# First layer of an audio tower: the attention's out-projection computed from high and low parts, with new steps on ScalarE, VectorE and TensorE

## The reference

```
h = tok(x)                                     # pairs of tokens -> 188 tokens, conv as a product, layer norm
h = h + attn0(layernorm(h))                    # 16 heads of 16; the softmax runs over the batch axis (64)
h = h + ffn0(layernorm(h))                     # 256 -> 704 -> 256, inputs, weights and hidden rounded to FP4 by blocks of 16
h = h + attn1(layernorm(h))                    # linear attention, 16 heads of 64
h = h + ffn1(h)                                # 256 -> 1024 -> 256, integer weights
# end of attn0:
out = out.transpose(1, 0, 2).reshape(L, N, inner)
out = einsum('lni,ei->lne', out, out_proj) + out_bias
```

## Time and profile before

| what | value |
|---|---|
| median of 3 runs | 4551.7 us (4547.76 to 4551.86) |
| the profiled execution's own time | 4539.33 us |
| its span in the profile | 4536.7 us |
| TensorE matmuls busy over the span | 4354.9 us, 96% |
| TensorE weight loads | 3972.3 us, 88% |
| DVE | 3317.8 us, 73% |
| ACT | 2712.1 us, 60% |
| POOL | 2100.0 us, 46% |

### The profile page before, as it was taken

One profiled execution on the slowest core, in us unless ns is written; L12 is line 12 of the kernel. 1 busy time (PEld: TensorE's weight loads), 2 busy tenths in 40 slices (PEclk: granted clock), 3 DMA queues, 4 the chain that ended last, 5 costly groups with the idle time before them and its releaser, 6 DMA issues.

```text
span 4536.7 us, 121660 instructions
## 1 busy us (share of the span) xinstructions
PE 4354.9 (96%) x43948; PEld 3972.3 (88%) x43948; DVE 3317.8 (73%) x7106; ACT 2712.1 (60%) x5662; POOL 2100.0 (46%) x2682
## 2 busy tenths in 40 slices
PE   5999999999999958999999999999999999999997
PEld 4889999999899848899999999999999999989996
DVE  6999999999999845666666666666666666666665
ACT  4777777777777734555555555555555555545553
POOL 4566666666666522433433443343343344334333
PEclk8999999999999979999999999999999999999998
DMA  2100000000000010000000000000000000000000
GB/s 71 43 24 24 24 24 24 23 22 24 24 24 24 21 45 5 5 15 8 9 15 9 9 12 12 9 11 13 9 9 15 9 9 14 10 9 8 15 5 11
DMA packets 64982, 79.21 MB, mean 17 GB/s; under 512 B 8800, under 2 KB 51168, under 8 KB 64480
## 3 DMA queue, kind: packets, MB, share of 16 engines
q1 hardware_dynamic: 64608, 74.07, 5.6%
HBM read 49.40 MB, written 24.64 MB: 16 GB/s over the span
## 4 chain that ended last, share of the span: by engine, by line
PE 56%; DVE 3%; issue 2%; ACT 1%; POOL 1%; ACTq 0%; DVEq 0%; POOLq 0%
PE bA L1093 11%; PE bA L1095 9%; PE bA L1094 9%; PE bS L1398 4%; PE bO L1420 3%; PE bA L1484 3%; PE bB L1093 2%; PE bB L1094 2%; PE bB L1384 2%; PE bB L1095 2%; PE bB L1383 2%; PE bA L1485 2%; PE bT L1436 2%; PE bO L1424 1%; PE bO L1429 1%
## 5 line engine op out<-in xcount | busy, mean ns | idle before, releaser
L1820 POOL TENSOR_TENSOR sqs_lo<-sq,sqs_hi 128x768 fp32r<-128x768 f32 x256 | 480.6, 1878 | 673.9 <-ACT sqs_hi L1535 670.1
L1634 DVE TENSOR_TENSOR qk_lo<-bA,qk_hi 128x384 fp32r<-128x384 f32 x512 | 284.3, 556 | 517.1 <-ACT qk_hi L1535 516.8
L1554 ACT ACTIVATE phi<-bB 128x768 f32<-128x768 f32 x256 | 207.4, 810 | 662.5 <-PE bB L1384 662.5
L1778 POOL TENSOR_TENSOR yT_lo<-tanh_y,yT_hi 128x384 fp32r<-128x384 f32 x256 | 259.3, 1013 | 545.0 <-ACT yT_hi L1535 545.0
L1535 ACT ACTIVATE qk_hi<-bA 128x384 fp32r<-128x384 f32 x512 | 251.9, 492 | 195.2 <-PE bA L1095 188.0
L1644 DVE TENSOR_TENSOR aT<-bS,mask 128x1024 f32<-128x1024 f32 x256 | 311.0, 1215 | 1.3 <-PE bS L1403 1.3
L1544 ACT ACTIVATE sq<-bA 128x384 f32<-128x384 f32 x512 | 250.2, 489 | 62.1 <-DVE qk_lo L1634 61.3
L571 ACT ACTIVATE kblk<-gu,kb_masked,rowmask 128x128 f32<-128x128 f32 x752 | 271.7, 465 | 5.1 <-PE gu L452 5.0
L1093 PE MATMUL bA<-fc_lo,yT_hi 128*128 128x256 f32 x768 | 230.7, 300 | 13.1 <-POOL yT_lo L1778 6.4
L1093 PE MATMUL bA<-wv_lo,xT_hi 128*128 128x256 f32 x768 | 230.0, 300 | 5.9 <-ACT sq L1544 1.3
L1093 PE MATMUL bA<-wo_lo,attT_hi 128*128 128x256 f32 x768 | 226.3, 295 | 9.8 <-ACT sq L1544 2.1
(11 more groups left out here) (269 smaller groups left out, 16222.6 us busy)
## 6 DMA issues: line engine op xcount, KB each, us to landing
xT<-in_x SPq DMA_DIRECT2D x94, 256.0 KB, 2.6
h_scratch<-h SPq DMA_DIRECT2D x188, 64.0 KB, 1.9
hx<-h_scratch SPq DMA_DIRECT2D x32, 256.0 KB, 2.7
out<-res SPq DMA_DIRECT2D x32, 256.0 KB, 2.2
hx<-h_scratch SPq DMA_DIRECT2D x64, 64.0 KB, 2.4
out<-res SPq DMA_DIRECT2D x64, 60.0 KB, 1.8
q<-in_fc_q SPq DMA_DIRECT2D x2, 1024.0 KB, 7.7
wq_sb<-in_wq SPq DMA_DIRECT2D x1, 1024.0 KB, 5.0
```

The source lines that it names most:

```text
L1634: dve.tensor_tensor(dst, src, hi.bitcast(fp32), ALU.subtract).then_inc(S[done], 1)
L1778: pool.tensor_tensor(yT[1][:, f % RING, :], tanh_y[f % 2][:], yT[0][:, f % RING, :].bitcast(fp32), ALU.subtract).then_inc(S["y_lo"], 1)
L1820: pool.tensor_tensor(sqs[1][:], sq[:], sqs[0][:].bitcast(fp32), ALU.subtract).then_inc(S["sq_lo"], 1)
```

## The change

`attT` becomes a pair, `attT_hi` and `attT_lo`, in fp32r, and so does the out-projection's weight, `outw_hi` and `outw_lo`, made once from `outw_sb`: the high part by ACT at the end of slot 0, the low part by DVE in slot 1. In every slot ACT's `att_copy` writes `attT_hi` and stands ahead of the tanh of half 0 in place of behind it. A new DVE step, `att_low`, subtracts it from the transposes in PSUM into `attT_lo`; it stands behind `score_shift` and ahead of `glu_gate` of half 0, and raises `attT_split`. The out-projection waits for `attT_split` and calls `product3` twice. All who waited for `attT_copied` to reuse the PSUM bank now wait for `attT_split`.

```
-        attT = sb("attT", [128, KC, 128])
+        attT = sb("attT_hi", [128, KC, 128], fp32r), sb("attT_lo", [128, KC, 128], fp32r)
+        outw = sb("outw_hi", [128, KC, DM], fp32r), sb("outw_lo", [128, KC, DM], fp32r)
...
 def xq_transpose(t):
-                              [("attT_copied", t - 3, 1, 1), ("xqT_split", t - 4, 1, 1)])
+                              [("attT_split", t - 3, 1, 1), ("xqT_split", t - 4, 1, 1)])
 def att_transpose(t):
-                              [("ln1T_copied", t - 1, 1, 1), ("attT_copied", t - 3, 1, 1)])
+                              [("ln1T_copied", t - 1, 1, 1), ("attT_split", t - 3, 1, 1)])
 def outproj(t):
-                    wait(pe, "attT_copied", t - 1)
+                    if isinstance(t, int) and t == 2:
+                        pe.wait_ge(wout_lo, 1)
+                    wait(pe, "attT_split", t - 1)
                     for c in range(KC):
-                        last = pe.matmul(cv[:, 0:DM], attT[:, c, :], outw_sb[:, c, :], start=c == 0, stop=c == KC - 1)
+                        last = product3(pe, cv[:, 0:DM], [x[:, c, :] for x in attT], [x[:, c, :] for x in outw],
+                                        c == 0, c == KC - 1)
 def ln1_transpose(t):
-                    bank_free(pe, t, [("attT_copied", t - 2, 1, 1)],
+                    bank_free(pe, t, [("attT_split", t - 2, 1, 1)],
...
 ACT, att_copy:
-                    copy(attT[:], tp[:, 0:256], "attT_copied")
+                    copy(attT[0][:], tp[:, 0:256].rearrange("p (c t) -> p c t", c=KC), "attT_copied")
 ACT, slot:
+                    if exists(t, 2):
+                        att_copy(t)
                     if exists(t, 3):
                         tanh(t - 3, 0)
-                    if exists(t, 2):
-                        att_copy(t)
                     if exists(t, 0):
                         ln0_normalize(t)
...
                     if isinstance(t, int) and t == 0:
+                        act.wait_ge(wout, 32)
+                        act.activation(outw[0][:], outw_sb[:], ACT.Copy).then_inc(wout_hi, 1)
                         weight_magnitude("up")
...
 DVE:
+                def att_low(t):
+                    wait(dve, "attT_copied", t - 1)
+                    dve.tensor_tensor(attT[1][:], tp[:, 0:256].rearrange("p (c t) -> p c t", c=KC), attT[0][:].bitcast(fp32),
+                                      ALU.subtract).then_inc(S["attT_split"], 1)
 DVE, slot:
                         score_shift(t - 1, s_st)
+                    if exists(t, 2):
+                        att_low(t)
                     if exists(t, 3):
                         glu_gate(t - 3, 0)
                         glu_up(t - 3, 0)
...
                     if isinstance(t, int) and t == 1:
+                        dve.wait_ge(wout_hi, 1)
+                        dve.tensor_tensor(outw[1][:], outw_sb[:], outw[0][:].bitcast(fp32), ALU.subtract).then_inc(wout_lo, 1)
                         dve.wait_ge(S["rs1"], 4 * 2)
                         weight_round("up")
```

## The result

The change made the kernel slower, by 0.6%. Its median is 4578.59 us (4577.03 to 4582.4, 4 runs) beside 4550.93 us for the kernel before (4547.76 to 4551.86, 4 runs): ratio 1.0063, interval 1.0046 to 1.0081, that is 27.7 us. The prediction had 22.7 us more and 4574.

A forecast was written before the change was run, and what follows sets the result against it. A tie between DVE's ring and TensorE's was taken to bound the kernel; 91 slots x 0.24 = 21.9, with slot 2 22.7 us more: 4562.0 from the profiled execution, 4574.4 from the median; 8 in 10 range 4558 to 4592.

The forecast's parts named there:

- DVE's ring: Loop slot: closed chain from `rowmax` through DVE, POOL, ACT and the scores back to `rowmax`; `att_low` adds net 0.24 us.
- The pitch and its cover: `att_low` on DVE: 0.34 us start to start, less 0.10 us covered by the wait for the up products.
- TensorE's saving: Out-projection: six fp32r products for four fp32 pieces save 0.16 us per tile, if TensorE waited for nothing.
- its new wait: TensorE waits for `att_low` before the out-projection, starting near 913.95 in place of 913.70; costs nothing beyond the ring.
- the other kind of slot: Slots where DVE waits for the up products; out-projection slips about 0.1 us, more than made good.
- ACT's order: `attT`'s copy ahead of tanh(0) delays `ln0_normalize` and what follows on ACT by 0.10 us, hidden: nothing.
- slot 2: Before the loop: TensorE waits for `att_low` behind `P`, so `up_hi` moves 0.8 us later; other end nothing.
- the weights: Splitting the out-projection weight on ACT in slot 0 and DVE in slot 1 fits in idle time: nothing.
- TensorE's busy share: Sign in the profile between 300 and 1500 us: down by about 2 points, with a new idle before `q_sb`.
- TensorE as the bound: Rival: DVE has room, so every tile saves 0.16 us, 15 us in all, 4537 us; chance 0.10.
- The tanh's delay: Rival: its 0.10 us on ACT comes on top, 31.7 us in all, 4583 us; chance 0.09.
- nothing to measure: Rival: hidden room or TensorE's saving leaves net 0 to 0.1 us per slot, 4551 to 4560 us; chance 0.11.

The follow-up runs named there:

- e1_subtract: The kernel before plus only DVE's subtraction into a tile nobody reads, out-projection still fp32: 4568.94 us, ratio 1.003, slot 16.634 us.
- e2_nolow: The changed kernel with `att_low` run in slot 2 alone, later slots reading a stale low part: 4552.68 us, ratio 0.9992, slot 16.402 us.
- e3_order: The kernel before with ACT's `att_copy` moved ahead of the first tanh, nothing else: 4554.28 us, ratio 0.9999, slot 16.417 us.
- e6_twice: `e1_subtract` with a second DVE subtraction into another tile behind the first: 4592.22 us, slot 16.975 us.
- e11_regap_nolow: `e2_nolow` with the two reorderings of `e9_regap_before`: 4529.2 us in one run, slot 16.282 us.
- e10_regap_after: The changed kernel with the reorderings of `e9_regap_before` and slot 2's `att_low` ahead of `rowmax`: 4549.47 us, ratio 1.0015, slot 16.396 us.
- e4_slot2: The changed kernel with `att_low` ahead of `rowmax` and `P` in slot 2 alone: 4580.03 us, ratio 1.0054.
- e7_more_pe: The kernel before with one fp32 out-projection product issued twice, 0.43 us more on TensorE per slot: 4590.4 us, slot 16.815 us.
- e9_regap_before: The kernel before with `hq_round` ahead of `xq_round` on DVE and `binade_x` between the `kblk` halves on ACT: 4540.16 us, ratio 0.9997, slot 16.378 us.
- e5_again: The kernel before, unchanged, profiled a second time: 4546.31 us, slot 16.401 us.
- e8_between: The changed kernel with `att_low` moved between the gate and up steps of half 0 on DVE: 4582.01 us, ratio 1.0087, slot 16.858 us.

## Why the prediction was right, and where it was off

**Direction and mechanism: right.** `att_low` lengthens DVE's ring, and with it that ring sets the slot. `e1_subtract` shows it alone makes the whole growth (16.634 against 16.633); `e2_nolow` and `e3_order` show that the other parts make none.

**The pitch and its cover: right.** Forecast 0.34 less 0.10; measured 0.33 to 0.34 (`e6_twice`) less 0.12, 0.218 in place of 0.24. The loop came to 20.3 us, not 21.9. (The prediction read the slot of before as 16.44 from a count of slots, where it is 16.415, and counted 91 slots, where the stores have 93 intervals.) The duration of 0.39 that the prediction worked out from the Trainium skill (VectorE: DVE Perf Modes, the section on TRN2 errata) lies between the row's length of 0.41 and its pitch of 0.33; as a price of the step it was too high, as the row had said.

**TensorE's saving uncounted, its new wait free: right in the slot, too hopeful on TensorE.** Counted from `P`, the out-projection was to start 0.25 later and did; the second gate product was to come 0.09 later and came 0.17 later. In the other kind of slot the saving was to more than make good the wait, and the product came 0.08 later there as well (2.65 in place of 2.57, mean of 35). The slot didn't feel it: `e1_subtract`, without that wait, has the same 16.63. The saving, forecast at 0.16, is 0.14 without a wait and 0.08 behind one. It is worth no more than 0.013 in `e2_nolow` and 0.10 in `e11_regap_nolow`, and with `attT_lo` computed it is gone (`e10_regap_after`).

**ACT's order costs nothing: right** (`e3_order`).

**The edges: slot 2 mis-sized.** Slot 2 had 0.8 us and the weights nothing. The first store came 2.9 us later, and slot 2 alone grew by 2.45. I had `up_hi`, the first copy of the transposes of `uraw`, 0.8 us later; counted from `rowmax` it came 1.77 later (66.89 - 61.58 in place of 64.90 - 61.36). The six products and the transposes ran at half the clock, which I hadn't thought of, and I followed the delay no further than that copy. The weights' low half took 1.06 us on DVE, but slot 1 grew by 0.1 only, within its scatter, so "nothing" stands. What would give the 2.9 back is not known: the first store is 1.2 later in `e1_subtract`, with slot 2's step but no weights, and 1.6 in `e2_nolow`, with the weights and slot 2's step. And `e4_slot2` shows that most of slot 2's stall can go without anything won at the first store.

**The loop's end: missing.** Nothing was forecast there, and it cost up to 3.8 us. I summed 91 equal slots without asking what happens where TensorE goes from looped to unrolled code. Rows for it were in the trace of before, a 2 us stall, unread.

**The sum.** 20.3 + 2.9 + 3.8 = 27.0 us beside 27.7 measured; the forecast was 21.9 + 0.8. The slot was 1.6 too high and the two edges 5.9 too low.

**The signs in the profile.** Right: the slot (16.63, forecast 16.68), the pitch, the products at 0.12 us (the first 0.19) with TensorE waiting before them, no wait for the up products, `binade_x` unchanged. Wrong: TensorE's busy share fell 0.7 of a point (weight loads 1.5), not 2, and no idle appeared before `q_sb`; the delay is taken up before the out-projection and the scores instead.

**The rivals.** TensorE as the bound would have had `e1_subtract` at no cost and `e2_nolow` 0.16 shorter; neither was so. Yet it stood nearer than its chance of 0.10 suggests: `e7_more_pe` and `e9_regap_before` put its ring 0.02 to 0.04 us under the slot. The tanh's delay falls with `e3_order`, and "nothing to measure" with the 0.218. The prediction named the Trainium skill's rule that weight-load time says more than matmul time (Perfetto Trace Analysis, "Identifying the Most-Contended Engine"). By it TensorE had 90% and DVE 91%, a tie, and near a tie is what the experiments found. As a measure of room it did not serve here: the weight loads leave 10% of the slot free, and 0.43 us more work on TensorE cost 0.40. The 0.4% that the matmuls leave was nearer to the 0.03 us that were there.

## What to carry to other kernels

Where two engines' rings are level, work moved from one to the other is paid on the one and not credited on the other: price it at start-to-start pitch less whatever wait it displaces (0.34 - 0.12 here), and test the tie by adding a known step to each engine in turn. When a producer and its consumer sit on different rings, the producer's place matters as much as its length: moving it 0.43 us later won 0.12 on DVE and lost 0.22 in the slot. Price the edges of a loop as well, since its first unrolled slots and its exit made a quarter of this loss.

## What the runs showed of the hardware that was not expected

- Where the loop ends TensorE's queue stands 2.1 us in one program and 3.9 to 4.2 us in another with no releaser named, and behind the longer stall the granted clock was 0.50 to 0.59 for 5 us. In `e5_again` it fell too, to 0.52 over 3 us, behind a stall of 2.07 us, while in the first profile of the same kernel, behind 2.09 us, it stayed at 1.00.
- The second layer, the same instructions in every kernel, took from 2884 to 2903 us (measured from its first load to the end of the span), so a single pair of profiles can't settle a difference of 10 us in this kernel. Slots and stores can.
- In slot 2 of the changed kernel TensorE stood 3.59 us and came back at a granted clock of 0.50, with products 0.21 us apart; in `e4_slot2` it stood 1.13 us there and came back at 1.00, with products 0.12 us apart. So the same six products took 1.42 us or 0.78.
- Two DVE steps of which the second doesn't read the first follow each other 0.1 us closer: gate to up took 0.54 us, gate to `att_low` 0.43 (`e8_between`).
